# Shared experts' opening reordered, and their deferred pieces as three rounded products

## What is computed

```
x = x + tanh(g_ffn[0]) * L0_ffn(layernorm(x))              # end of block 0: two gathered rows per token, weighted
...
x = x + tanh(g_xattn[1]) * (LN(LN(x) + summary) * gamma + beta)
h  = silu(xb @ Wg) * (xb @ Wu);  yb = h @ Wd               # 64 routed experts, 128 tokens each
hs = silu(flat @ Sg) * (flat @ Su)                         # 2 shared experts
out = scatter_add(yb * w) + einsum('nsh,shd->nd', hs, Sd)  # the shared experts' way back
```

## Time and profile before

| | us |
|---|---|
| median of three runs | 1121.69 |
| lowest, highest | 1120.41, 1123.66 |
| the profiled execution, its own time | 1124.97 |
| its span in the trace | 1123.2 |
| busy PE, weight loads, DVE, ACT, POOL | 1028.6, 739.4, 723.4, 500.6, 589.3 |
| `experts` stage in the trace | 842.6 to 1123.2 |

### The profile page before, as it was taken

The page is one execution under the profiler, slowest core; times in us unless marked ns, Lnnn a source line. Parts: engine busy times, 40 slices in busy tenths (PEclk is TensorE's granted clock), DMA queues, the critical chain, the costliest instruction groups (busy, mean ns, idle before and its releaser), DMA issues. The chain is left out here.

```text
span 1123.2 us, 18838 instructions
## 1 busy us (share of the span) xinstructions
PE 1028.6 (92%) x5364; PEld 739.4 (66%) x5364; DVE 723.4 (64%) x1703; ACT 500.6 (45%) x880; POOL 589.3 (52%) x556
## 2 busy tenths in 40 slices
PE   5899999999869999998899999999989999999950
PEld 3456555565327777775289478577768888888840
DVE  4577787876448888886688248267316666666650
ACT  3466566565338888886432201311313333333320
POOL 6466766775416676675534646356432344333541
PEclk8999999999989999999899999999999999999985
DMA  9976555773544332332540241043269999999638
GB/s 289 342 228 201 171 180 191 240 246 104 197 150 152 111 105 102 112 103 75 181 144 20 87 140 44 11 136 112 87 209 345 333 323 313 277 331 336 160 70 149
DMA packets 128254, 199.49 MB, mean 178 GB/s; under 512 B 35975, under 2 KB 44167, under 8 KB 128186
## 3 DMA queue, kind: packets, MB, share of 16 engines
q1 hardware_dynamic: 106538, 160.66, 42.7%
q0 software_dynamic: 21360, 37.48, 13.2%
q10 hardware_dynamic: 288, 0.52, 0.1%
HBM read 133.10 MB, written 87.56 MB: 196 GB/s over the span
## 5 line engine op out<-in xcount | busy, mean ns | idle before, releaser
L935 POOL TENSOR_TENSOR m_down_lo<-wo,m_down_hi 128x512 fp32r<-128x512 f32 x78 | 129.8, 1683 | 74.9 <-ACT m_down_hi L1030 74.9
L543 PE MATMUL bank<-win,vT 128*128 128x512 f32 x256 | 124.5, 600 | 0.0
L703 DVE TENSOR_REDUCE negmax<-bank 128x1 bf16<-128x512 f32 x128 | 85.6, 672 | 43.2 <-PE bank L550 42.8
L633 ACT ACTIVATE win<-bank 128x512 f32<-128x512 f32 x128 | 69.4, 594 | 90.1 <-PE bank L535 86.3
L1044 DVE TENSOR_TENSOR m_up_lo<-w,m_up_hi 128x1024 fp32r<-128x1024 f32 x78 | 96.8, 1242 | 13.1 <-ACT m_up_hi L1002 11.8
L2034 POOL DMA_INDIRECT out<-m_y,m_token x32 | 50.9, 1590 | 91.2 <-DMA out<-m_y,m_token 61.5
L1264 POOL DMA_INDIRECT tab<-stage_up,slot x64 | 65.9, 1029 | 53.4 <-DVE slot L1610 35.5
L2064 PE MATMUL bank<-y,m_w 128*128 128x128 f32 x736 | 89.7, 275 | 0.0
L2178 ACT ACTIVATE sh_gate_a<-bank 128x512 f32<-128x512 f32 (+1 forms) x40 | 20.5, 513 | 150.8 <-PE bank L2171 120.6
L2034 POOL DMA_INDIRECT sums<-m_y,m_token x32 | 51.2, 1599 | 69.2 <-DVE m_y L2128 41.3
L2064 PEld LDWEIGHTS bank<-y,m_w 128*128 128x128 f32 x736 | 86.4, 193 | 0.1
(11 more groups left out here) (297 smaller groups left out, 2503.9 us busy)
## 6 DMA issues: line engine op xcount, KB each, us to landing
tab<-zeros SPq DMA_DIRECT2D x16, 1056.0 KB
m_w<-in_L_ffn_Wg SPq DMA_DIRECT2D x46, 256.0 KB
m_w<-in_L_ffn_Wu SPq DMA_DIRECT2D x46, 256.0 KB
m_w<-in_L_ffn_Wd SPq DMA_DIRECT2D x46, 256.0 KB
m_x<-tab SPq DMA_DIRECT2D x39, 256.0 KB, 2.6
ytab<-m_y SPq DMA_DIRECT2D x39, 256.0 KB, 2.1
stage_up<-tab SPq DMA_DIRECT2D x32, 264.0 KB
m_x<-tab SPq DMA_DIRECT2D x32, 264.0 KB
```

What stands on the lines that cost most here:

```text
L543: nc.tensor.matmul(pO[s * 2 + h][:], vT[:, s, sb_, h:h + 2, :].rearrange("p a c -> p (a c)"), probs[:, sb_ % 2, h, :], start=(sb_ == 0), s ...
L633: nc.scalar.activation(probs[:, b % 2, h, :], pS[h][:], ACT.Exp, scale=1.0 / HEAD).then_inc(p_ready, 1)
L703: nc.vector.tensor_reduce(negmax[:, s, m:m + 1], rough_bank(k, m)[:], AX.X, ALU.max, negate=True).then_inc(pm_read, 1)
L935: nc.gpsimd.tensor_tensor(dn_lo[:, m, :], row(wo0, e * MB + m), dn_hi[:, m, :], ALU.subtract).then_inc(dn_lo_ready, 1)
```

## The change

1. `gather(0, ...)` on GpSimd: the gathers of tile 2 come behind the first root and those of tile 3 behind the second, where all four tiles' gathers stood ahead of the first root.
2. On PE, the residual matmul of a tile is taken out of `mixed(j)` and issued earlier, without the wait for the gathered rows: tiles 0 and 1 at the start, tile 2 ahead of `with_beta(0)`, tile 3 behind the summary rows. `mixed(1)` comes ahead of `summary_row(0)`.
3. Each deferred piece (one f32 matmul) becomes three fp32r matmuls. Two steps ahead, ACT rounds a half of the hidden values (128x128) and, for the first eight pieces, a 128x512 block of the weights; DVE makes the low parts of both. PE waits for them. The low weights take the place of the f32 weights in memory, the high ones the place of `flat_hi` and `flat_lo`.
4. Some semaphores are joined; the waits mean the same.

```diff
+            gather(0, (0, 1))
+            inverse_std(first_stat(0, 0), 0, 2)
+            gather(0, (2,))
+            inverse_std(first_stat(0, 1), 0, 2)
+            gather(0, (3,))
+            inverse_std(first_stat(0, 2), 0, 2)
-            gather(0, range(TPB))
-            for k in range(3):
-                inverse_std(first_stat(0, k), 0, 2)
...
+            def before_mixture(j):
+                if j == 3:
+                    pe.wait_ge(x3_ready, 1)
+                nc.tensor.matmul(x2_bank[j][:], ident[:], x_sb[:, j, :], start=True, stop=False)
             def mixed(j):
                 pe.wait_ge(diag_ready, j + 1)
                 pe.wait_ge(gathered[j], 16 * 2)
-                if j == 3:
-                    pe.wait_ge(x3_ready, 1)
-                nc.tensor.matmul(x2_bank[j][:], ident[:], x_sb[:, j, :], start=True, stop=False)
...
             def first_steps():
+                before_mixture(0)
+                before_mixture(1)
                 mixed(0)
+                mixed(1)
                 summary_row(0)
-                mixed(1)
                 summary_row(1)
+                before_mixture(2)
                 with_beta(0)
                 with_beta(1)
                 mixed(2)
                 summary_row(2)
                 summary_row(3)
+                before_mixture(3)
                 mixed(3)
...
@@ experts, tensor
-                        last = nc.tensor.matmul(pB[j % 2][:], (late_hidden if j < LATE else hidden)[:, n, tile * P:tile * P + P],
-                                                w_sd[:, n // (HSH // P), n % (HSH // P), :],
-                                                start=(n == 0), stop=(n == CHUNKS - 1))
+                        k, ws, wb, _ = piece(i)
+                        pe.wait_ge(back_lo_ready, k + 1)
+                        for part, (a, w) in enumerate(((back_hi, w_sd_hi), (back_lo, w_sd_hi), (back_hi, w_sd_lo))):
+                            last = nc.tensor.matmul(pB[j % 2][:], a[:, k % 2, :], w[:, ws, wb, :],
+                                                    start=(n == 0 and part == 0), stop=(n == CHUNKS - 1 and part == 2))
+                        last.then_inc(back_used, 1)
@@ experts, scalar, behind the rounding of the down weights
+                    if back_at(i + 2):
+                        k, ws, wb, half = piece(i + 2)
+                        if k < CHUNKS:
+                            nc.scalar.copy(w_sd_hi[:, ws, wb, :], w_sd[:, ws, wb, :])
+                        need(act, back_used, k - 1)
+                        nc.scalar.copy(back_hi[:, k % 2, :], half).then_inc(back_hi_ready, 1)
@@ experts, vector, behind y of expert i-1
+                if i < E1 and back_at(i + 2):
+                    k, ws, wb, half = piece(i + 2)
+                    dve.wait_ge(back_hi_ready, k + 1)
+                    if k < CHUNKS:
+                        nc.vector.tensor_tensor(w_sd_lo[:, ws, wb, :], w_sd[:, ws, wb, :], w_sd_hi[:, ws, wb, :], ALU.subtract)
+                    nc.vector.tensor_tensor(back_lo[:, k % 2, :], half, back_hi[:, k % 2, :],
+                                            ALU.subtract).then_inc(back_lo_ready, 1)
```

More of the change, by code:

```diff
@@ L154, in build @@
                 T["s_w1"] = [staged.enter_context(nc.semaphore(f"m1_loaded_{n}")) for n in range(W_RING)]
-                T["w_sd"] = sb("w_sd", [P, NSH, DB, HSH], F32, later, "right")
-                T["flat_hi"], T["flat_lo"] = (sb(n, [P, DB, SEQ], F32R, later, "right") for n in ("flat_hi", "flat_lo"))
+                whole = ExitStack()
+                T["w_sd"] = sb("w_sd", [P, NSH, DB, HSH], F32, whole, "right")
+                T["flat_hi"], T["flat_lo"] = (sb(n, [P, DB, SEQ], F32R, whole, "right") for n in ("flat_hi", "flat_lo"))
+                whole.close()
+                T["w_sd_lo"], T["w_sd_hi"] = (sb(n, [P, NSH, DB, HSH], F32R, later, "right") for n in ("w_sd_lo", "w_sd_hi"))
                 splits = ExitStack()
@@ L1973, in experts @@
         h_hi, h_lo = (sb(f"m1_h_{n}", [P, 2, CAP1], F32R) for n in ("hi", "lo"))
+        back_hi, back_lo = (sb(f"shared_back_{n}", [P, 2, P], F32R) for n in ("hi", "lo"))
+        w_sd_hi, w_sd_lo = T["w_sd_hi"], T["w_sd_lo"]
+        back_hi_ready, back_lo_ready, back_used = sem("shared_back_hi_ready"), sem("shared_back_lo_ready"), sem("shared_back_used")
         y = sb("m1_y", [P, RING, D])
@@ L1979, in experts @@
         down_hi_ready, down_lo_ready = sem("m1_down_hi_ready"), sem("m1_down_lo_ready")
-        back_full, back_read = sem("shared_back_full"), sem("shared_back_read")
+        back_read = sem("shared_back_read")
         pX, pH, pY, pB = bank[0:2], bank[2:4], bank[4:6], bank[6:8]
@@ L1989, in experts @@
         rest = T["summary"]
-        rest_loaded, rest_ready, stored = sem("rest_loaded"), sem("rest_ready"), sem("out_stored")
+        rest_loaded, joined = sem("rest_loaded"), added[0]
         block = c.enter_context(nc.Block())
@@ L1995, in back_at, with piece @@
             return divmod(i - BACK, CHUNKS) if 0 <= i - BACK < (LATE + TPB) * CHUNKS else None
+        def piece(i):
+            j, n = back_at(i)
+            tile = (AT_ONCE + j) % TPB
+            return i - BACK, n // (HSH // P), n % (HSH // P), (late_hidden if j < LATE else hidden)[:, n, tile * P:tile * P + P]
         def entries(e):
@@ L2040, in _ @@
             for n in range(PARTS - 1):
-                nc.gpsimd.dma_start(whole[n], part[n], max_dma_last_dim=2 * 4 * D, accum_op=ALU.add).then_inc(stored, 16)
-            pool.wait_ge(rest_ready, 1)
+                nc.gpsimd.dma_start(whole[n], part[n], max_dma_last_dim=2 * 4 * D, accum_op=ALU.add).then_inc(joined, 16)
+            pool.wait_ge(back_read, LATE + TPB + 1)
             nc.gpsimd.dma_start(T["out_rows"].rearrange("(t p) d -> p t d", p=P)[:, TILES - TPB:, :], rest[:],
-                                accum_op=ALU.add).then_inc(stored, 16)
-            pool.wait_ge(stored, 16 * PARTS)
+                                accum_op=ALU.add).then_inc(joined, 16)
+            pool.wait_ge(joined, 16 * E1 // SUMS + 16 * PARTS)
         @block.tensor
@@ L2070, in _ @@
                             need(pe, back_read, j - 1)
-                        tile = (AT_ONCE + j) % TPB
-                        last = nc.tensor.matmul(pB[j % 2][:], (late_hidden if j < LATE else hidden)[:, n, tile * P:tile * P + P],
-                                                w_sd[:, n // (HSH // P), n % (HSH // P), :],
-                                                start=(n == 0), stop=(n == CHUNKS - 1))
-                        if n == CHUNKS - 1:
-                            last.then_inc(back_full, 1)
+                        k, ws, wb, _ = piece(i)
[4 more added lines that the diff above has]
+                        last.then_inc(back_used, 1)
                 if valid(i - 1, n=E1):
@@ L2129, in _ @@
                                             ALU.mult).then_inc(y_ready, 1)
+                if i < E1 and back_at(i + 2):
[5 more added lines that the diff above has]
+                                            ALU.subtract).then_inc(back_lo_ready, 1)
                 if back_at(i - 1) and back_at(i - 1)[1] == CHUNKS - 1:
                     j = back_at(i - 1)[0]
-                    dve.wait_ge(back_full, j + 1)
+                    dve.wait_ge(back_used, CHUNKS * (j + 1))
                     if j == 0:
@@ L2137, in _ @@
             dve.wait_ge(rest_loaded, 16)
-            nc.vector.tensor_tensor(rest[:], rest[:], x_sb[:, TILES - TPB:, :], ALU.add).then_inc(rest_ready, 1)
+            nc.vector.tensor_tensor(rest[:], rest[:], x_sb[:, TILES - TPB:, :], ALU.add).then_inc(back_read, 1)
 class SharedExperts:
```

## The result

The changed kernel takes 1124.13 us, median of 20 runs (1118.84 to 1128.56). The kernel before, in 20 runs on the same chip, takes 1120.81 (1116.12 to 1125.51). The ratio is 1.0031, with a 95% interval of 1.0017 to 1.0044: 3.3 us slower, where 2.7 us less had been forecast. The two parts of the change went different ways. The deferred pieces did about what was forecast.

What follows compares the result with a forecast made beforehand. PE, without gaps, and the adds to `out` were taken to bound `experts` almost together. Of PE's 8.4 us plus the opening's 1.0, 2.7 would arrive: 1121.69 - 2.7 = 1119.0 us, 8-in-10 range 1112 to 1124.5.

Steps and rivals of the forecast that it cites:

- The piece: PE in `experts`: three products take 0.70 instead of 0.86 us, 0.15 less per piece, 8.4 us over 56 pieces.
- DVE: In `experts`: busy 3.0 of 3.66 us per step, mostly hidden; cost to PE 0 to 3 us, taken as 1.5.
- The chain of adds: POOL's successive adds to `out` become the bound in `experts`; last add at 1085.8 against 1088.49, 2.7 us gained.
- the lag: Delay of POOL's add to `out` behind its ready y: some 20 us at expert 49, hidden by eight buffers.
- The links under load: Time from one add to `out` to the next while loads run: 7.52 us, later 7.73, taken as 7.5 and 7.7.
- The join: In `experts`, issued after expert 31's add lands: forecast at 977.5, with the next add to `out` at 988.8.
- The rival of denser loads: In `experts`, faster PE keeps DMA full: 8.08 us between adds, last add at 1094, time 1127.3; chance 0.12.
- Two signs: In `experts`: adds to `out` wait for their table nearly all along; y always finds one of eight buffers free.
- The opening: First tiles, up to the first shared product: 1.0 us earlier, bounds 1.8 earlier to 0.5 later.
- a similar hole: PE wait ahead of tile 2's mixture; a low clock on matmuls behind it would take the opening's gain back.
- products no shorter: Rival on PE: weight load shows or DVE holds PE, only the opening's 1.0 us is left, 1120.7; chance 0.10.
- PE's gain whole: Rival in `experts`: PE's saving arrives in full, gain 9.4 us with the opening, 1112.3; chance 0.20.

Runs made afterwards that it cites:

- e1: Kernel before with only the deferred pieces as three rounded products, opening as before: ratio 0.9982 to the kernel before, 1124.42 against 1126.95 us.
- e7: Kernel before with each add to `out` carrying 256 of 512 columns (half the routed result left out): ratio 0.9987 to the kernel before, 1118.69 us.
- e8: Three rounded products, opening of before, each add to `out` carrying 256 of 512 columns: ratio 0.9926 to the kernel before, 1111.49 us.
- e10: Changed kernel unaltered, run again on another call: ratio 1.0035 to the kernel before, 1130.46 us.
- e2: Kernel before with only the new opening (both its parts), pieces still f32: ratio 1.0068 to the kernel before, 1134.22 against 1126.95 us.
- e3: Kernel before with only PE's new opening order, POOL's gathers as before, f32 pieces: ratio 0.9998 to the kernel before.
- e4: Kernel before with only the gathers of tiles 2 and 3 behind the roots, PE's order as before, f32 pieces: ratio 1.0013 to the kernel before.
- e12: Changed kernel with tile 2's gathers back ahead of the first root and tile 3's ahead of the second: ratio 0.9956 to the kernel before, 1122.87 us.
- e11: Three rounded products, PE's old opening order, gathers of tiles 0 to 2 ahead of the first root, tile 3's behind it: ratio 0.9963 to the kernel before.
- e6: New opening with f32 pieces, and the 2 MB gate weight load held until tile 3's rows landed: ratio 1.0111 to the kernel before.
- e9: Changed kernel with three idle f32 matmuls behind `with_beta(1)`, where PE waits for tile 2's rows: ratio 0.9982 to the kernel before, 1126.05 us.

## Why the prediction was right or wrong

**The piece: right in sum, by half from where it was reckoned.** 0.15 us less each, a period of 3.66 and 9.4 us for the last y (8.4 + 1.0) were forecast. The period is 3.66 and the last y came 9.0 earlier. But the working gave all of it to the three products, and piece and down products together are only 0.08 us shorter (1.48 against 1.56): the second and third product come 0.23 apart, as the neighbours' price of 0.235 said, but the first takes 0.32. (The 893.77 from which the f32 piece was priced is a reckoned start: the trace of before has the first down product from 893.37, inside the piece's records.) The other 0.08 came from the transposes, gate and up ahead of the piece (2.18 against 2.26), which nobody touched; why isn't shown. That the two add up to the forecast is luck. So is part of the 9.0: counted from the first transposes of the stage the last y came 10.0 us earlier, of which 1.5 is the slow first gate and up in before's profile, and the stage started 1.0 later instead of 1.0 earlier. By the four passes that the Trainium skill gives to a full FP32 product ("FP8 and Floating Point Precision", TensorE Precision Notes) a period would have become 3.61 (an estimate); measured is 3.66.

**DVE: right.** 3.0 of 3.66 us per step were forecast; 69.50 / 84 x 3.66 is 3.03. The 1.5 us that it was to cost PE didn't come: in this stage PE waited for DVE once, for 1.8 us, and for 1.9 before.

**The chain of adds: right in kind, and close in size.** The share of PE's saving that arrives was put at 1.7 of 8.4 us. In the profiles the stage is 2.4 shorter (243.4 against 245.9, each rounded), with 1.5 of before's being the slow first gate and up; e1's median says 2.5 us, with zero just inside its interval. Over all profiles with whole adds the stage takes 240.2 to 244.2 with products, 242.1 as the mean of six, and 244.4 to 245.9 with f32 pieces, 244.8 as the mean of six, so some 2.6 us less. e7 and e8 show that it is the adds that hold back the rest, and the lag of 20.5 us at expert 49 is the one that was forecast (some 20). The single terms were less exact. The links under load had been put at 7.5 and 7.7. The nine of experts 3 to 21 took (936.07 - 864.74) / 9 = 7.93 (before 7.52, e10 7.67), the seven of experts 33 to 47 took (1045.83 - 992.19) / 7 = 7.66. The join came at 980.77 instead of 977.5, the next add at 992.19 instead of 988.8, and expert 47's at 1045.83 instead of 1042.1: 3.7 late. The eight links from there to the last add were put at 43.7 us and took 1087.09 - 1045.83 = 41.3. Errors of +3.7 and -2.4 thus left the last add at 1087.09, where 1085.8 was expected; that they nearly cancel is luck. The rival of denser loads had the longer links right, but they reached neither its 8.08 nor the end of the stage.

Two signs didn't come. Adds to `out` were to wait for their table nearly all along; it was 18 of 32 times and 52.7 us, less than the 20 times and 61.5 of the earlier trace rows, while the adds to `sums` waited for theirs 35.2 us instead of 22.7 (POOL issues both in one order). And y was to find a free buffer always. The waits of the changed kernel from 790 us on:

```profile
POOL out L2056 <- DMA out<-m_y,m_token: 52.7, 18, 4.9
...
DVE m_y L2156 <- DMA out<-m_y,m_token: 4.5, 5, 1.5
```

The eight buffers were used up five times, for 4.5 us in all.

**The opening: wrong, and with it the sign.** The first half of the step held: the first root was forecast for 547.2 and came at 547.04. The step that failed is the next, the hole ahead of tile 2's mixture. The prediction named it ("a similar hole") but gave it no length, let it cost at most the gain plus 0.5, and reckoned a landing only for tile 3's gathers, with "the 2.5 us that tile 1's took to land". That 2.5 came from a gather issued by 538.90, before the gate load (542.36 in the trace of before). Tile 2's last gather is issued 11.5 us later, into DMA engines at a share of 1.05, and took 5.2; for tile 3's PE never waited. Moving a DMA behind a root didn't only put it later, it put it beside a 2 MB load. Nothing in the earlier trace rows measured the landing of a gather there, and I should have bounded it by both. In the earlier trace rows the adds, indirect DMAs of the same size, take 7.5 us per link beside loads and 5.46 without; that was the row to take for the upper end.

The second error is the size of what the clock costs in that hole. The rows at the low clock took 3.75, 3.78, 2.08 and 3.38 us for what takes about 1.88, 1.98, 1.12 and 1.88, which is 6.1 us more. With the 2.7 us by which tile 2's rows landed later than 2.5 us would have had them that is 8.8, where the opening missed its forecast by 7.7; the rest had slack. So the term is -1.0 as forecast, +6.7 in the profile, and +5.5 to +6 in the runs of e1 and the changed kernel.

**The sum.** With the opening worked out in this way (+6.7) and the adds as forecast (-1.7) the sum would have been +5.0 us, where +3.3 was measured. By the two halves run apart it is -2.5 (e1) + 7.3 (e2) = +4.8, and the intervals are wide enough for the difference. The range of 1112 to 1124.5 held 1124.13 by a hair and by luck: its upper end came from longer links of the adds, not from the opening. Of the rivals, two fell with e1, e7 and e8: products no shorter (the period is), PE's gain whole (only with half the bytes in the adds).

What stays open: why e3 and e4, each alone, cost 0.4 and 1.2 us by the medians and together 7.3; what decides whether the clock falls at beta (the other twelve profiles) or only in the wait behind it (changed, e10); and whether e12's 5.0 us (by the ratio) owe anything to its opening beyond e1's, since the intervals of e1, e11 and e12 overlap.

## What to carry to other kernels

When an issue of a DMA is moved, price its landing by what else the DMA engines carry at the new time, not by the row at the old one, and then ask what its consumer does in the wait: on PE a hole of some microseconds costs the work behind it a second time, through the clock. When an engine without gaps is made faster, look for the chain that keeps pace with it by a hair; here 8.4 us on PE became about 2.5 until the adds were halved. And one profile per kernel can hide a difference of some microseconds that lies elsewhere, so compare stages from their own starts and let the runs give the sum.

## What the runs showed of the hardware

- The rows of a tile (two gathers of 128 rows) released PE 2.7 us after the issue of the second with the load held (e6), and 5.1 to 5.3 us with the load running (e2, changed kernel, e10).
- In the changed kernel PE waited for 4.69 us. The granted clock was full in the first part of the wait, fell before its end, and stayed at 1.2 GHz for about 12 us of work behind it. In e4, with a wait of 2.44, the slow records ended four to five after it. In e12 the clock was at its low level at the beta matmuls and came back while PE went on without a wait; in e9 the same, with the filler in the wait.
- Three matmuls that compute nothing, in the place of the wait, made the kernel 4.4 us faster (e9 against e10).
- The same stretch of untouched code, from the first transposed tile to `experts`, took 275.4 to 283.4 us in fourteen profiles.
